# Two chained 3x3 convolutions: the second layer runs one chunk further behind the first, the input ring goes from 4 slots to 3, and the second layer's weights are built at another place

## What is computed

```python
def _gn(v, G=8, eps=1e-5):
    g = v.reshape(B_, G, C_ // G, H_, W_)
    m = jnp.mean(g, axis=(2, 3, 4), keepdims=True)
    s = jnp.var(g, axis=(2, 3, 4), keepdims=True)
    return ((g - m) / jnp.sqrt(s + eps)).reshape(v.shape)
...
# --- layer 0: weights rotated per image by an angle from its statistics; zero padding
x = x + _L0_conv_ref(_gn(x), L0_conv_w_fft_real, L0_conv_w_fft_imag, ...)
# --- layer 1: a convolution by FFT, so with circular padding
x = x + _L1_conv_ref(_gn(x), L1_conv_weight)
```

## Time and profile before

| | us |
|---|---|
| median of 3 runs | 1865.82 |
| lowest and highest run | 1863.42, 1867.4 |
| the profiled execution, its own time | 1864.99 |
| its span in the profile | 1863.2 |
| TensorE busy (of the span) | 1665.9 (89%) |
| VectorE busy | 1446.1 (78%) |
| ScalarE busy | 1134.3 (61%) |
| GpSimd busy | 80.8 (4%) |
| mean share of the DMA queue of SyncE | 62.2% |

### The profile page before, as it was taken

One profiled execution on the slowest core, in us unless ns is written; L12 is line 12 of the kernel. 1 busy time (PEld: TensorE's weight loads), 2 busy tenths in 40 slices (PEclk: granted clock), 3 DMA queues, 4 the chain that ended last, 5 costly groups with the idle time before them and its releaser, 6 DMA issues.

```text
span 1863.2 us, 65217 instructions
## 1 busy us (share of the span) xinstructions
PE 1665.9 (89%) x29275; PEld 1246.1 (67%) x29275; DVE 1446.1 (78%) x2291; ACT 1134.3 (61%) x944; POOL 80.8 (4%) x261
## 2 busy tenths in 40 slices
PE   6888888276679998999999899989998999899899
PEld 5778887133345555887688668866785668566766
DVE  6889999589987887778787878787878787877700
ACT  6887888235546665665666566656665666566434
POOL 0000000200010000000000000000000000000100
PEclk9999999689989999999999999999999999999999
DMA  9999999144436655665666556556665666566245
GB/s 387 421 422 422 422 421 421 38 131 134 129 114 206 203 196 173 210 199 161 206 201 202 183 173 225 198 175 205 208 197 164 207 200 200 171 205 205 118 175 205
DMA packets 101974, 411.57 MB, mean 221 GB/s; under 512 B 17139, under 2 KB 19688, under 8 KB 85352
## 3 DMA queue, kind: packets, MB, share of 16 engines
q1 hardware_dynamic: 101064, 407.88, 62.2%
q0 software_dynamic: 672, 0.08, 0.1%
HBM read 271.82 MB, written 136.07 MB: 219 GB/s over the span
## 4 chain that ended last, share of the span: by engine, by line
PE 66%; DVE 22%; issue 6%; DMA 5%; ACT 1%; SPq 1%; DVEq 0%; POOL 0%; ACTq 0%; POOLq 0%
PE ps L376 33%; PE ps L369 31%; DVE x L577 6%; DMA x<-x_pix 5%; DVE nat L796 3%; DVE stats L844 3%; DVE x L809 2%; DVE sm L881 1%; ACT x L445 1%; PE ps L320 0%; PE ps L321 0%; DVE sm L921 0%; DVE ps L815 0%; PE ps L328 0%; DVE sm L922 0%
## 5 line engine op out<-in xcount | busy, mean ns | idle before, releaser
L369 PE MATMUL ps<-nat,wc 64*64 64x512 f16 (+1 forms) x12480 | 1280.0, 381 | 96.2 <-DVE nat L796 40.6
L376 PE MATMUL ps<-x,wc 64*64 64x512 f16 (+2 forms) x12585 | 1265.2, 377 | 7.6 <-issue 7.1
L369 PEld LDWEIGHTS ps<-nat,wc 64*64 64x64 f16 x12480 | 725.1, 108 | 309.8 <-issue 78.8
L376 PEld LDWEIGHTS ps<-x,wc 64*64 64x64 f16 x12585 | 737.9, 107 | 188.2 <-issue 8.9
L467 ACT ACTIVATE nat<-xin,gnp 128x1024 f16<-128x1024 f32 (+1 forms) x264 | 299.7, 1136 | 335.3 <-PE ps L369 321.2
L477 ACT ACTIVATE x<-ps,gnp 128x1024 f16<-128x1024 f32 (+1 forms) x264 | 289.7, 1097 | 214.3 <-DVE stats L844 214.2
L488 ACT ACTIVATE outb<-ps,bias 128x1024 f32<-128x1024 f32 (+1 forms) x264 | 289.5, 1097 | 86.0 <-PE ps L376 71.8
L809 DVE SCALAR_TENSOR_TENSOR x<-ps,gnp,x 128x1024 f16<-128x1024 f32 (+1 forms) x264 | 333.1, 1262 | 6.1 <-ACT x L477 5.9
L844 DVE BATCH_NORM_STATS2 stats<-ps 128x6 f32<-128x512 f32 (+1 forms) x520 | 335.9, 687 | 0.1
L796 DVE SCALAR_TENSOR_TENSOR nat<-xin,gnp,nat 128x1024 f16<-128x1024 f32 (+1 forms) x264 | 331.8, 1257 | 1.8 <-ACT nat L467 1.6
L320 PE MATMUL ps<-x 128*128 128x129 f16 x2048 | 257.4, 226 | 60.0 <-DVE x L577 59.8
(11 more groups left out here) (134 smaller groups left out, 196.6 us busy)
## 6 DMA issues: line engine op xcount, KB each, us to landing
x<-x_pix SPq DMA_DIRECT2D x128, 1024.0 KB, 13.6
xin<-x_tiles SPq DMA_DIRECT2D x256, 512.0 KB, 3.8
out<-outb SPq DMA_DIRECT2D x256, 512.0 KB, 4.1
xin<-x_tiles SPq DMA_DIRECT2D x8, 192.5 KB, 2.4
out<-outb SPq DMA_DIRECT2D x8, 192.5 KB, 3.5
w<-taps_scratch SPq DMA_DIRECT2D x64, 8.0 KB, 1.8
w<-taps_scratch SPq DMA_DIRECT2D x32, 16.0 KB, 2.4
taps_scratch<-x POOLq DMA_DIRECT2D x21, 3.0 KB, 2.0
```

The source lines that it names most:

```text
L369: return nc.tensor.matmul(ps[64 * kind:64 * kind + 64, bank, 0:w], lhs, nat[rows, xhl, a:a + w], start=first, stop=last)
L376: ins = nc.tensor.matmul(ps[64 * kind:64 * kind + 64, bank, done:done + part], lhs, x1[rows, xhl, z:z + part], start=first and done == 0, ...
```

## The change

Four numbers move: `LAG` from 35 to 36 chunks, the ring `x1` from 37 to 38 chunks (`RING`), and the input ring `xin` from 4 to 3 slots (`NI`, new). `nat` keeps its 4 slots. So a load waits for the `lo0` three chunks back instead of four, and the SyncE queue's turn g holds `load_x(g + 7)` instead of `load_x(g + 8)`, behind the same `lo0(g + 4)`. At the start three chunks are loaded ahead, and `pad(3)` and `pad(4)` stand between the first calls of `lo0`. `weights1` of an image leaves the turn of its last chunk and follows `lo1` of the next image's first chunk; for the last image it comes after the loop's last layer 0 turn, which is the same place in VectorE's queue as before.

```diff
 NX = 4
+NI = 3
...
-LAG = NCH + 2
-RING = NCH + 4
+LAG = NCH + 3
+RING = NCH + 5
...
-        xin = sb("xin", [P, NX, CH])
+        xin = sb("xin", [P, NI, CH])
...
-                if g >= NX:
-                    sp.wait_ge(lo0_ready, g - NX + 1)
-                sp.dma_start(xin[:, g % NX, 0:writes(n)], x_tiles[b, :, n * CH:n * CH + writes(n)]
-                             ).then_inc(x_in[g % NX], 16)
-
-            for g in range(NX):
+                if g >= NI:
+                    sp.wait_ge(lo0_ready, g - NI + 1)
+                sp.dma_start(xin[:, g % NI, 0:writes(n)], x_tiles[b, :, n * CH:n * CH + writes(n)]
+                             ).then_inc(x_in[g % NI], 16)
+
+            for g in range(NI):
                 load_x(g)
...
-            for g in range(NX, 2 * NX):
+            for g in range(NI, NX + NI):
                 load_x(g)
             for g in range(ALL + LAG):
                 b, n = divmod(g, NCH)
-                if g + 2 * NX < ALL:
-                    load_x(g + 2 * NX)
+                if g + NX + NI < ALL:
+                    load_x(g + NX + NI)
...
-            for g in range(NX):
+            for g in range(NI):
                 pad(g)
             for part in range(4):
                 weights0(0, part)
             for g in range(NX):
                 lo0(g)
-            pad(NX)
+                if g + NI <= NX:
+                    pad(g + NI)
             for g in range(ALL + LAG):
...
+                if g == ALL:
+                    weights1(B - 1)
                 if g >= ALL:
                     continue
...
                     spread(b)
-                    weights1(b)
                     if b > 0 and g + NX < ALL:
                         lo0(g + NX)
                 else:
                     if g + NX < ALL:
                         lo0(g + NX)
                     lo1(g)
+                    if n == 0 and b > 0:
+                        weights1(b - 1)
```

More of the change, by code:

```diff
@@ L172, in conv_program @@
         taps_rest = sem("taps_rest")
-        x_in = [sem(f"x_in{s}") for s in range(NX)]
+        x_in = [sem(f"x_in{s}") for s in range(NI)]
         w_in = sem("w_in")
@@ L466, in hi0 @@
                     act.wait_ge(pe_done, JOB0[g - NX] + 1)
-                nc.scalar.activation(nat[:, 0, (g % NX) * CH:(g % NX) * CH + w], xin[:, g % NX, 0:w], ACT.Identity,
+                nc.scalar.activation(nat[:, 0, (g % NX) * CH:(g % NX) * CH + w], xin[:, g % NI, 0:w], ACT.Identity,
                                      scale=gnp[:, 1, b:b + 1]).then_inc(hi0_ready, 1)
@@ L776, in pad @@
                 mean = gnp[:, 0, b:b + 1]
-                slot = xin[:, g % NX, :]
-                ve.wait_ge(x_in[g % NX], 16 * (g // NX + 1))
+                slot = xin[:, g % NI, :]
+                ve.wait_ge(x_in[g % NI], 16 * (g // NI + 1))
                 if n == 0:
@@ L795, in lo0 @@
                 ve.wait_ge(hi0_ready, g + 1)
-                ins = V.scalar_tensor_tensor(nat[:, 1, a:a + w], xin[:, g % NX, 0:w], gnp[:, 1, b:b + 1],
+                ins = V.scalar_tensor_tensor(nat[:, 1, a:a + w], xin[:, g % NI, 0:w], gnp[:, 1, b:b + 1],
                                              nat[:, 0, a:a + w], ALU.mult, ALU.subtract)
```

## The result

| | before | after |
|---|---|---|
| median, us | 1865.82 (5 runs, 1863.42 to 1867.96) | 1855.91 (5 runs, 1854.75 to 1861.79) |
| the profiled execution, its own time | 1864.99 | 1854.76 |
| its span in the profile | 1863.2 | 1852.9 |

After over before is 0.995, with a 95% interval of 0.9931 to 0.9969: faster by 0.3 to 0.7%. A second series of the same kernel on another chip gave 1857.43 (6 runs, 1855.59 to 1859.65), 0.9965 (0.9954 to 0.9977) of before. The forecast was 1852, from a sum of -13.9 us; the span of the profiled execution is 10.3 us shorter.

A forecast was written before the change was run, and what follows sets the result against it. VectorE paces layer 0 alone, TensorE the mixed stage, losing time in image-boundary gaps and the slow clock behind. Terms 3.8 + 2.8 + 0 - 0.6 - 15.8 - 4.1 = -13.9 us gave 1852 us; range 1845 to 1862.

The forecast's parts named there:

- 1, the first loads: Start: with three slots load 3 waits for `lo0(0)`, so TensorE starts later, at 380.3; +3.8 us.
- 2, the small transfers: Layer 0 stage: VectorE waits at one pad for the x load behind 12 small DMAs; +2.8 us.
- 3, the mixed stage: Images 1 to 6, both layers: late x loads make VectorE wait, but existing slack covers it; 0, bounds 0 to +3.
- C: Rival: three input slots starve the layer 0 stage, pads of chunks 8 to 36 wait; slower, 1873 us; chance 0.05.
- 4, one more chunk of lag: Before the mixed stage: +1.3 us for one more chunk at VectorE's pace, 1.9 of slow clock given back; net -0.6.
- 5, images 1 to 6: Image boundaries: gap shrinks from 4.7 to 3.0 us and about half the clock loss goes; -2.6 each, -15.8 together.
- A: Rival: the clock still falls for as long as before at every boundary; 1861 us; chance 0.15.
- B: Rival: the clock no longer falls at most boundaries; 1846 us; chance 0.14.
- sure part: Boundaries of images 1 to 6: TensorE resumes 1.73 us earlier because `lo1(99)` comes earlier; 6 x 1.73 = 10.4 us.
- The bound of -21: Images 1 to 6 together: the largest gain allowed, if none of the shortened gaps still counted as long for the clock.
- 6, the last image: Last boundary: one more layer 1 job cuts the gap from 4.20 to 1.6 us and the slow clock goes; -4.1 us.
- D: Rival: the boundary doesn't yield, something else is late right behind `lo1(99)`; 1868 us, no measurable change; chance 0.11.

The follow-up runs named there:

- the cut kernels: VectorE's end-of-image work parted over turns 0 and 1: on the changed kernel 1850.25 us; with chunks 3, 4 loaded ahead and small DMAs spread too, 1843.88 us.

## Why the prediction was right in sign and range, and where its steps were off

**1, the first loads: right.** +3.76 and +3.46 us against +3.8, by the mechanism named: TensorE starts at 379.96, forecast 380.3, and 6.61 us behind the start of `lo0(0)` instead of 2.90. The second load's wait was covered, as said. Loading two chunks ahead takes the waits away.

**2, the small transfers: right place, half the price, and a sum that came out by luck.** The wait was to be 2.8 us and is 1.43 and 1.92. The pad came 3.8 us later than in the earlier trace rows, with the start. I had the load of x come later by as much, but it came only 2.8 us later (431.84 instead of 429.03, since the twelve DMAs took 6.33 us instead of 7.28), and it landed in 3.6 us where I had 4.0: 2.8 - 1.0 - 0.4 = 1.4. That the stage still cost 2.34 and 2.85 us is the other 0.92, the clock behind the gap of 3.73 us, which the forecast doesn't have. The spread DMAs take 2.0 us away, which is the wait of 1.92 in the series beside them.

**3, the mixed stage: right.** VectorE waits for `xin` in three places, 0.23 to 0.92 us, and TensorE idles at none of them. C, the starved layer 0 stage, didn't come about.

**4, one more chunk of lag: the jobs are counted right, the clock given back is not there.** By marks -3.2 us were due before chunk 64, and -0.92 came. Of this, -1.3 (3.88 for the chunk at VectorE's pace, less 5.2 for a pair of jobs) is the count of jobs, and it stands. What failed is the 1.9 us of slow clock given back. In this stretch the clock hardly touches the time: with lag 36 and the undivided work six profiles take 176.91 to 176.93 us from the mark of chunk 31 to that of 64, at a granted clock of 0.82 to 0.91 over the first 40 us. Two of them, the changed kernel in both series:

```profile
520.20:560.20 40.00, 25.27 (x386) 13.50 (x390) 34.28 (x84) 14.93 (x15) 4.76 (x12) 0.91 0.34 103
520.41:560.41 40.00, 27.30 (x386) 14.11 (x390) 34.29 (x84) 15.11 (x15) 4.77 (x12) 0.83 0.35 103
```

Where the clock is higher, TensorE is busy for 2.0 us less and idles for 2.0 us more. And before the change there was little to give back: the four kernels with lag 35 that build image 0's weights in the old place take 177.39 and 177.51 us at 0.87, 177.60 and 177.84 at 0.79. The other 0.4 us may be the two pairs of jobs that VectorE still paces; no run measures them apart.

**5, images 1 to 6: -13.9 and -11.5 against -15.8.** The gap shrank to 3.0 us as said, and the clock was right as an estimate of half: it fell at half of the boundaries, so neither A nor B came about: the images lost 1.0 us each to it in the first profile and 1.4 in the second (means of the table above), of some 2 before. What was mis-sized is the "sure part". At the same level, 0.83 before and after (image 5), an image gained 1.15 us and not 1.73. The half microsecond that goes with the 36th chunk was missing; the run with that chunk and without the move shows it, and with lag 35 the same image gained 1.67. The bound of -21 isn't a sum of what stands beside it (six times 1.73 + 2.0 is 22.4, and 18.8 with the 0.6 that may wait in its place); with the clock wholly kept, the cut kernels gave -19.8. And "nothing shown lies between" 1.2 and 4.2 us held for the rows, not for the trace: the gap of 3.73 us of the layer 0 stage stands in it, with a clock of 0.83 over the 10 us behind.

The page "TensorE: Matmul & The Clock Gate" of the Trainium skill, section "HAM oscillation — how this bites in real kernels", has the gate close at each idle gap that is long enough. The rows here agree for gaps of 4.2 us and more and for those of 1.8 and less; at 3.0 us both results stand side by side in one execution.

**6, the last image: right.** The gap went from 4.20 to 1.51 us and the slow clock from 0.85 to 1.00, both as said, and by marks the end gave -1.58 and -1.57 us against -1.5. All of it is the clock. The job of layer 1 that fills the gap moves nothing here: from `lo1(263)` to the first matmul behind the gap it is 6.15 us before and 6.14 after, and the jobs behind it are the same ones. Its 2.6 us are earned upstream, ahead of chunk 64, where the measured stage falls short for the reason under 4. Terms 4 and 6 together were -4.7 in the sum and are -2.5.

The misses are 1.9 and 4.3 us in the images and 2.3 on the way into the mixed stage, less 0.1 at the end and less 0.5 and 0.3 by which the start and the layer 0 stage cost less than forecast. Together they are the 3.6 and 6.2 us between the sum of -13.9 and the -10.3 and -7.7 of the two profiles. D didn't occur: the boundary yielded.

## What to carry to other kernels

- A forecast's terms and the marks by which it is measured have to cut the program at the same places. Here the two terms of the longer lag sum to -4.7 us and the program gave -2.5, but which of them failed shows only when the jobs between each pair of marks are counted.
- A slow clock can be given back only where TensorE sets the time. In a stage that VectorE paces, a faster TensorE waits for longer.
- When a gap on TensorE can't be removed, cut it. The same 3.5 us of idle time in one piece and two crumbs cost up to 3 us more an image than in two pieces, because of the clock behind it. And look at which other number makes the cut possible: here it is the lag, which by itself only costs.
- Few numbers of a short series say something about such a kernel: two series of one kernel lay 1.5 us apart, and the profile shows which images made it.

## What the runs showed of the hardware that I had not expected

**A gap of one length with two outcomes.** Behind 2.95 to 3.29 us of idle TensorE, between stretches of full work, the granted clock over the next 10 us was 1.00 in 16 of 48 cases, 0.83 to 0.87 in most others and 0.70 to 0.72 in the rest; both in one execution, and not tied to the image. With lag 36 half of them kept the clock, with lag 35 one of 18; but three of the five profiles with lag 36 show one and the same pattern, so these are fewer cases than they seem, and whether the lag matters, which changes only the order of the jobs near the gap, is open. Behind 3.73 us in the layer 0 stage it fell in 13 of 14 profiles. Two gaps of 1.4 to 1.8 us, 5.6 to 5.8 us from start to start, never lowered it (12 pairs in two kernels).

**Twelve small DMAs in a row** (8 and 16 KB each) held SyncE's queue for 6.3 to 7.3 us in the layer 0 stage. Two of them beside a load of x took 0.84 us in four of six turns and 2.44 and 2.62 in the others, and no load of x came late.
